# Convolution and gated feed-forward on one core: gate and up weights transposed by DMA, and the convolution's rows rounded on ScalarE

## What is computed

```python
K = 2.0 * einsum('hn,hnl->hl', Ct, exp(P)).real        # one long filter per head, length 1024
y = irfft(rfft(x) * rfft(K)) + x * D                    # causal convolution
y = y * (arange(L) < length)                            # mask
def qlinear(x, w):                                      # both sides rounded to 8-bit levels
    s = max(abs(t)) / 127; q = round(t / s) * s         # per row of x, per output row of w
    return einsum('bsh,oh->bso', xq, wq)
out = x + qlinear(silu(qlinear(y, w_gate)) * qlinear(y, w_up), w_down)
```

## Time and profile before

| what | value |
|---|---|
| median of 3 runs | 1317.04 us |
| the profiled execution | 1316.23 us |
| its span in the trace | 1313.0 us |
| TensorE busy | 1242.5 us, 95% |
| VectorE busy | 915.2 us, 70% |
| ScalarE busy | 408.7 us, 31% |
| GpSimd busy | 339.5 us, 26% |
| packets of the DMA queue, as a share of 16 engines | 45.3% of the span |

### The profile page before, as it was taken

The page is one execution under the profiler, slowest core; times in us unless marked ns, Lnnn a source line. Parts: engine busy times, 40 slices in busy tenths (PEclk is TensorE's granted clock), DMA queues, the critical chain, the costliest instruction groups (busy, mean ns, idle before and its releaser), DMA issues.

```text
span 1313.0 us, 19670 instructions
## 1 busy us (share of the span) xinstructions
PE 1242.5 (95%) x6581; PEld 675.8 (51%) x6676; DVE 915.2 (70%) x1542; ACT 408.7 (31%) x595; POOL 339.5 (26%) x318
## 2 busy tenths in 40 slices
PE   2499999999997999999999999999999999999997
PEld 0377777776763444444444444444444444444443
DVE  7578888888876577765677755677756677756675
ACT  2244454445531322222322222222222222222222
POOL 2133344325530321121221121221121221122220
PEclk9999999999998999999999999999999999999999
DMA  3279999998962233322223322323322323322322
GB/s 100 86 227 283 288 278 296 290 300 251 305 211 83 43 72 78 86 62 70 69 69 78 86 62 70 70 68 81 83 62 70 70 68 83 81 62 70 70 63 78
DMA packets 137593, 161.51 MB, mean 123 GB/s; under 512 B 101644, under 2 KB 101854, under 8 KB 136286
## 3 DMA queue, kind: packets, MB, share of 16 engines
q1 hardware_dynamic: 137566, 161.16, 45.3%
HBM read 113.28 MB, written 25.49 MB: 106 GB/s over the span
## 4 chain that ended last, share of the span: by engine, by line
PE 68%; issue 0%; DVE 0%; ACT 0%
PE ps_g L1055 23%; PE ps_u L1055 23%; PE ps_o L1081 22%; PE ps_o L1088 1%; PE ps_t L1065 0%; ACT h_t L1190 0%; DVE ps_o L1142 0%; DVE res L1145 0%
## 5 line engine op out<-in xcount | busy, mean ns | idle before, releaser
L1219 POOL TENSOR_TENSOR h_int<-h,rounder 128x512 bf16<-128x512 f32 x186 | 174.4, 952 | 703.3 <-ACT h L1181 700.6
L1055 PE MATMUL ps_g<-wgu,rows 128*128 128x512 bf16 (+1 forms) x1516 | 327.1, 358 | 5.9 <-PEq L405 4.9
L1055 PE MATMUL ps_u<-wgu,rows 128*128 128x512 bf16 (+1 forms) x1493 | 324.7, 357 | 2.3
L1081 PE MATMUL ps_o<-wd,h_t 128*128 128x512 bf16 x1314 | 294.0, 379 | 1.8 <-issue 0.2
L1175 ACT ACTIVATE g_buf<-g_buf 128x512 f32<-128x512 f32 x192 | 112.3, 585 | 584.1 <-DVE g_buf L1113 584.1
L1113 DVE SCALAR_TENSOR_TENSOR g_buf<-ps_g,sx_all,wide 128x512 f32<-128x512 f32 x192 | 132.3, 689 | 229.6 <-PE ps_g L1055 229.6
L846 PE MATMUL ps_y<-u,toep 128*128 128x512 f32 (+7 forms) x1024 | 266.2, 413 | 2.3 <-ACT s_rows L715 0.9
L1055 PEld LDWEIGHTS ps_g<-wgu,rows 128*128 128x128 bf16 x1536 | 145.2, 98 | 163.5 <-issue 13.2
L1055 PEld LDWEIGHTS ps_u<-wgu,rows 128*128 128x128 bf16 x1536 | 147.1, 98 | 151.8 <-issue 1.4
L846 PEld LDWEIGHTS ps_y<-u,toep 128*128 128x128 f32 x1024 | 177.6, 192 | 89.6 <-issue 57.5
L1081 PEld LDWEIGHTS ps_o<-wd,h_t 128*128 128x128 bf16 x1346 | 131.0, 98 | 151.9 <-issue 1.1
(11 more groups left out here) (140 smaller groups left out, 623.1 us busy)
## 6 DMA issues: line engine op xcount, KB each, us to landing
toep<-k_rev SPq DMA_DIRECT2D x64, 512.0 KB, 6.4
res<-in_x SPq DMA_DIRECT2D x64, 256.0 KB, 3.9
out_x<-res SPq DMA_DIRECT2D x64, 256.0 KB, 3.2
wide<-in_L_ffn_w_gate SPq DMA_DIRECT2D x22, 512.0 KB, 6.8
wide<-in_L_ffn_w_up SPq DMA_DIRECT2D x22, 512.0 KB, 8.7
wide<-in_L_ffn_w_down SPq DMA_DIRECT2D x8, 1376.0 KB, 7.5
rows<-in_x SPq DMA_DIRECT2D x32, 256.0 KB, 6.8
x_more<-in_x SPq DMA_DIRECT2D x32, 256.0 KB, 7.0
```

Of the source, the lines that this page charges most:

```text
L1055: last = pe.matmul(bank[:, 0:n], xq[:, par, c, :], wgu[:, NC - 1 - c, first + cols.start:first + cols.stop], start=(c == 0), stop=(c == NC ...
L1081: last = pe.matmul(ps_o[o][:], h_t[0:width, c, :], wd[0:width, c, o * W:(o + 1) * W], start=(c == 0), stop=(c == FC - 1))
L1219: pool.tensor_tensor(h_int[:, piece(j)], h[:, par, piece(j)], rounder[:].to_broadcast([P, n]), ALU.subtract).then_inc(h_int_ready, 1)
```

## The change

Gate and up weights: the 16 transposes of TensorE in each gate iteration and the two ScalarE copies (L863, L676) go. In their place SyncE issues two DMA transposes (`move_w`), each of one half of `w_int` (128 x 1024 bf16, eight blocks, 256 KB) straight into `wgu`. Each is put ahead of the load of the same half for iteration i+2. GpSimd waits for the DMA's semaphore `w_moved[k]` in place of TensorE's. The down weights are handled as before, with piece numbers of their own.

Output rows of the convolution: VectorE keeps the multiplication (`y_scaled`) and loses the rounding. ScalarE does it in two steps (`round_y`): `y + ROUND` in place, 128 x 1024 f32, then `- ROUND` into `xq`. They stand last in ScalarE's iteration.

```diff
+            def move_w(i, k):
+                sp.wait_ge(w_int_ready, pieces(i, k) + 1)
+                first = row_of(i) + k * F
+                sp.dma_start_transpose(wgu[:, :, first:first + P], w_int[:, k * L:(k + 1) * L]).then_inc(w_moved[k], 16)
+
             def body(i, par):
                 if gate_stage(i):
+                    move_w(i, 0)
                     if has(i, GU_ITERS - 2):
-                        sp.wait_ge(w_int_ready, pieces(i, 0) + 1)
                         load_gu(i + 2, par, 0)
...
-                if gate_stage(i) and has(i, GU_ITERS - 2):
-                    sp.wait_ge(w_int_ready, pieces(i, 1) + 1)
-                    load_gu(i + 2, par, 1)
+                if gate_stage(i):
+                    move_w(i, 1)
+                    if has(i, GU_ITERS - 2):
+                        load_gu(i + 2, par, 1)
...
+            for k in range(2):
+                sp.wait_ge(w_moved[k], 16 * GU_ITERS)
...
-                if turned is not None:
-                    pool.wait_ge(w_turned, turned)
+                if gate_stage(i):
+                    if not isinstance(i, int) or i >= 1:
+                        pool.wait_ge(w_moved[k], 16 * i)
...
+            def round_y(i, par):
+                v = y[:, par].rearrange("p c h b -> p (c h b)")
+                act.wait_ge(y_scaled, i + 1)
+                act.activation(v, v, ACT.Copy, bias=ROUND).then_inc(y_rounded, 1)
+                act.wait_ge(y_rounded, i + 1)
+                if not isinstance(i, int) or i >= 1:
+                    act.wait_ge(xq_stored, 16 * i)
+                act.activation(xq[:].rearrange("p c t -> p (c t)"), v, ACT.Copy, bias=-ROUND).then_inc(xq_ready, 1)
...
             def place_w(i, par, k):
-                act.wait_ge(w_turned, pieces(i, k) + 1)
-                if gate_stage(i):
-                    dst = wgu[:, :, bass.ds(row_of(i) + k * F, P)]
-                    act.activation(dst, ps_w[k][:], ACT.Copy).then_inc(w_placed, 1)
-                    return
+                act.wait_ge(w_turned, down_pieces(i, k) + 1)
...
+                if not isinstance(i, int) or i >= 1:
+                    round_y(i - 1, 1 - par)
...
                 dve.tensor_tensor(v, v, ps_i[:].unsqueeze(1).to_broadcast([P, NC, P]), ALU.mult).then_inc(y_scaled, 1)
-                dve.wait_ge(y_scaled, i + 1)
-                if not isinstance(i, int) or i >= 1:
-                    dve.wait_ge(xq_stored, 16 * i)
-                dve.tensor_scalar(xq[:], v, ROUND, ROUND, ALU.add, ALU.subtract).then_inc(xq_ready, 1)
...
-                    if gate_stage(i) or down_stage(i):
-                        turn_w(i, par, hh if gate_stage(i) else 2 * hh)
+                    if not gate_stage(i) and down_stage(i):
+                        turn_w(i, par, 2 * hh)
```

More of the change, by code:

```diff
@@ L453, in convolve_and_pack @@
         w_int_ready = sem("w_int_ready")
+        w_moved = [sem(f"w_moved{k}") for k in range(2)]
         w_turned = sem("w_turned")
@@ L517, in run @@
             stage[0] = "down"
[L518 to L521, removed]
+            body(DOWN_FIRST, DOWN_FIRST % 2)
+            with eng.Fori(DOWN_FIRST + 1, WEIGHT_ITERS - 4, 2) as i:
+                body(i, 1 - DOWN_FIRST % 2)
+                body(i + 1, DOWN_FIRST % 2)
+            for i in range(WEIGHT_ITERS - 3, TILES):
                 body(i, i % 2)
@@ L606, in store_scales @@
                     sp.wait_ge(s_stored, 80)
-            run(sp, body, lambda: store_scales(0))
+            for i in range(DOWN_FIRST):
+                body(i, i % 2)
+            store_scales(0)
+            for k in range(2):
+                sp.wait_ge(w_moved[k], 16 * GU_ITERS)
+            for i in range(DOWN_FIRST, TILES):
+                body(i, i % 2)
             sp.wait_ge(xq_stored, 16 * TILES)
@@ L623, in unround @@
                     src, out = w_f32[:, down_half(par)][:, cols], w_int[:, cols]
-                if turned is not None:
-                    pool.wait_ge(w_turned, turned)
+                if gate_stage(i):
+                    if not isinstance(i, int) or i >= 1:
+                        pool.wait_ge(w_moved[k], 16 * i)
+                else:
+                    if k < 2 and isinstance(i, int) and i == DOWN_FIRST:
+                        pool.wait_ge(w_moved[k], 16 * GU_ITERS)
+                    if not isinstance(i, int) or i > DOWN_FIRST:
+                        pool.wait_ge(w_turned, down_pieces(i - 1, k) + 1)
                 if not gate_stage(i) and k == BATCHES - 1:
@@ L630, in unround @@
                                    ALU.subtract).then_inc(w_int_ready, 1)
-            unround(0, 0, 0, None)
+            unround(0, 0, 0)
             def body(i, par):
                 if gate_stage(i):
[L636 to L644, removed]
+                    unround(i, par, 1)
+                    if has(i, GU_ITERS - 1):
+                        unround(i + 1, 1 - par, 0)
+                else:
+                    if down_stage(i):
+                        unround(i, par, 2)
+                    if has(i, WEIGHT_ITERS - 1):
+                        unround(i + 1, 1 - par, 0)
+                        unround(i + 1, 1 - par, 1)
             run(pool, body)
@@ L721, in _ @@
             run(act, body)
+            round_y(TILES - 1, (TILES - 1) % 2)
         @block.vector
@@ L850, in turn_w @@
             def turn_w(i, par, k):
[L852 to L853 removed]
+                m = down_pieces(i, k)
+                pe.wait_ge(w_int_ready, pieces(i, k) + 1)
                 if not isinstance(i, int) or m >= 2:
                     pe.wait_ge(w_placed, m - 1)
[L857 to L861 removed]
+                cols = turn_cols(k)
+                bank, start, stop = ps_w[(BATCHES * down_slot(par) + k) % 2], cols.start, cols.stop
                 for c, f in enumerate(range(start, stop, P)):
@@ L891, in body @@
                             turn_x(1 - par, k)
-                    if gate_stage(i) or down_stage(i):
-                        turn_w(i, par, hh if gate_stage(i) else 2 * hh)
-                        if hh == 0 and not gate_stage(i):
+                    if not gate_stage(i) and down_stage(i):
+                        turn_w(i, par, 2 * hh)
+                        if hh == 0:
                             turn_w(i, par, 1)
```

19 lines of the change are left out of this document (4 added, 15 removed).

## The result

| | before | after |
|---|---|---|
| median | 1316.22 us (4 runs, 1314.43 to 1324.29) | 1330.03 us (4 runs, 1328.06 to 1330.83) |
| ratio after / before, 95% interval | | 1.0095 (1.0056 to 1.0133) |
| span of the profiled execution | 1313.0 us | 1328.2 us |

The change costs 14 us by the medians, and 7 to 18 us by the interval of the ratio. I had forecast 1362, at least 1332. The sign was right, the size was wrong by a factor of three. And the loss isn't where I put it.

What follows compares the result with a forecast made beforehand. TensorE sets the gate stage's pace and the DMA engines barely keep up; transposes +46.6 us, load margins -3, stage end +2.2, down stage 0: +45.8 us, giving 1362 us, range 1332 to 1404.

Steps and rivals of the forecast that it cites:

- The engines have 0.2 us of room, so the period grows to 10.05 + 2.65 - 0.2 = 12.5 us: Gate stage: DMA engines nearly full, so two transposes lengthen each of iterations 3 to 21, 46.6 us in all.
- Only that no wait shows: Gate stage: the only evidence named for room in the DMA queue, on which a faster kernel (1300.6 us, chance 0.07) rested.
- The draw: Gate stage rival: the queue gives some, the period stays at 10.05 us, 1319 us in all; chance 0.05.
- the sign that I had named against myself: Gate stage: a period under 10.1 us in the changed profile would prove the forecast wrong on the queue.
- The price of a transpose: Gate stage: 0.166 us of all DMA engines a block, so 2.65 us for the 16 blocks added to each iteration.
- The removed 0.89 us is therefore worth nothing: Gate stage: TensorE's saving in each iteration brings no time, as it waits for loads in the longer period.
- ScalarE has room, and `xq` 1.5 us later only shrinks SyncE's pause: Each iteration: ScalarE, busy 51.55 of 100.82 us, can take the rounding; later `xq` only shortens SyncE's 5.5 us pause.
- The down stage keeps its work: 0: Down stage, behind the gate iterations: the change was booked as costing no time there.
- The tail, +2.2: End of the down stage, tile 31: two rounding steps and a wait for tile 30's store add 2.2 us.
- The clock: Gate stage rival: idle TensorE runs slow convolutions, two an iteration, +101 us, 1417 us; chance 0.05.
- The range: Whole kernel: 1332 to 1404 us, taking in the lower transpose price and dearer transposes, leaving out the other rivals.
- The least price of the transposes: Gate stage: lower end, their bytes at 285 GB/s, 1.84 us an iteration, +31 us.

Runs made afterwards that it cites:

- e7: Kernel before plus two DMA transposes of `w_int` into the still unused `wd` in each gate iteration, nothing removed; 1320.8 us, ratio 1.0019.
- e2: Kernel before with only the DMA transposes of the change, the rounding left on VectorE in one step; 1319.6 us, ratio 1.0001.
- e5: Changed kernel with each DMA transpose issued twice, the first of the two into `wd`, GpSimd waiting for both; 1415.8 us, ratio 1.0738.
- e4: Changed kernel with the loads of `x` put ahead of the first transpose on SyncE's queue in the gate stage; 1330.2 us, ratio 1.0082.
- e3: Kernel before with only the rounding moved to ScalarE, the transposes left on TensorE; 1332.7 us, ratio 1.0104.
- e9: Kernel before with only the rounding moved to ScalarE, and the `s_rows` scale copies put ahead of it; 1323.4 us, ratio 1.0051.
- e1: Changed kernel with the `s_rows` scale copies put ahead of `round_y` on ScalarE in iterations 22 and 30; 1324.2 us, ratio 1.0037.
- e10: Changed kernel with ScalarE rounding only tiles 0 to 21 and VectorE rounding tiles 22 to 31; 1319.7 us, ratio 1.0017.

## Why the prediction was wrong

- **"The engines have 0.2 us of room, so the period grows to 10.05 + 2.65 - 0.2 = 12.5 us"** is the step that failed. The period stayed at 10.0 to 10.1, and e7 shows the room by itself: two more transposes, the same period. 46.6 us fell away. I had read a share of 1.00 as full, and the landings of 7 to 9 us as a backlog. The engines then moved 331 to 338 GB/s in three kernels. Over such a stretch the share went to 1.08 or 1.09 and no further, at 338 and at 301 GB/s. "Only that no wait shows" was what I held to speak for room, and it was the best evidence there was. The page "SBUF — State Buffer" of the Trainium skill (A bandwidth-pool intuition that's wrong) gives 436 GB/s for DMA traffic on the on-chip memory. No long stretch here came to it, and the highest slice of the profile after is 349; but the 1.87 us from 289.33 on moved 429 GB/s in the changed kernel, so the figure isn't out of reach. It would have warned me that 285 need not be full.
- **"The draw", 0.05**, was what the gate stage did, with its own number: it "needs 339 GB/s", and the windows show 336. Its mechanism, that the queue gives some and TensorE's saving is spent, is what came, as did the sign that I had named against myself, a period under 10.1 us. That its 1319 us is within 1 us of e2 is luck: the 2 us in it were for ScalarE's rounding at the end, which e2 hasn't, and e2 came there by a gain of 3.1 and a loss of 7.2 us.
- **The price of a transpose**: 1.33 us was an engine time, and in the period it was nothing where queue and SyncE had room (e7) and 2 us where SyncE had no pause left (e5). The issue was put at 1.23 us; it was 1.23 to 3.55 us in the changed kernel. Of SyncE I had said "no bound", and in e5 its issues fill the period. At the stage's end a long issue stood ahead of a load of `x`, for a 3 us wait. The prediction also read the page "DMA: Bandwidth & Descriptors" of the Trainium skill (Latency and other measured facts) as speaking of the destination; the page says "non-contiguous mid-dim" and not on which side. No run here tells the two kinds apart.
- **"The removed 0.89 us is therefore worth nothing"**: right, but for another reason. 0.79 and 0.49 us of waits for `x` took it, and where those were moved away (e4) a late gate load took it by way of VectorE. In the first iterations, which I had called cheap, some of it came through, for 3 us.
- **ScalarE has room, and `xq` 1.5 us later only shrinks SyncE's pause**: right in the gate stage (5.5 us became 2.7), wrong in the down stage. I counted ScalarE's busy time (half of a stretch of the gate stage) and didn't follow its order: the rounding waits for VectorE, and what stands behind it waits too. Two copies of 0.25 us were worth 7 to 9 us (e3 against e9, by ratios and by medians).
- **"The down stage keeps its work: 0"**: its work, yes. It measured +19.0 us, 8.8 of them by the order of the copies (e1 against after), most of the rest by later `x`.
- **The tail, +2.2**: 15.75 us from the last convolution's start to the next stage for 15.27 before, +0.5.
- **The clock** was a rival for the gate stage. It came in single places and not once an iteration: the two slow convolutions of 7.1 us, as the earlier trace rows had one, that of 5.80 us at 257.98, and the transposes and the convolution behind the wait of 3.03 us.
- **The range** had no case in which a cost lies outside the gate stage. The least price of the transposes, their bytes at 285 GB/s (+31 us), gives 1347; the end at 1332 lies 15 us below that and has no sum of its own. That the transposes could be free in time and the loss lie elsewhere had no case, and that 1330.03 came near that end is luck.

## What to carry to other kernels

A DMA share near 1.00 with long landings and no waits is no proof of a full queue; ask with extra transfers that nobody needs, and look whether the engine that issues them still has pauses. When an engine gets an operation that waits for another engine, look at each thing that stands behind it in its program, in every stage and in the rare iterations above all; its busy share says nothing on that. A time saved in a stage with several limits near each other is spent by the next one, and the order of loads at the joint of two stages is worth a look by itself.

## What the hardware showed that I had not expected

- An operation of VectorE beside one of GpSimd stretches: the `diag` step took 1.98 us at 186.84, beside GpSimd's of 1.89 that began at the same time, and takes 0.29 us alone. In e2 the rounding took 1.60 us for 0.69, begun 0.85 us behind one of GpSimd's of 1.89 us:

```profile
191.70 1.60 DVE L805 TENSOR_SCALAR xq<-y 128x1024 bf16<-128x1024 f32 x1
```

  The page "SBUF — State Buffer" of the Trainium skill (SBUF: two separate sides) says that some forms of VectorE operations and GpSimd share a pair of ports that one of them holds for a whole instruction. The trace agrees for these two forms: both ended within 0.6 us of GpSimd's end. VectorE's `tensor_tensor` ahead of the rounding, which also lay beside GpSimd's, kept its 1.21 us.
- A share of 1.07 to 1.09 stood beside 273, 301, 331 and 338 GB/s.
- The issue of a DMA transpose took SyncE between 1.23 and 4.60 us over all runs. Its length goes with the distance from the start of the transpose ahead: in e7, mostly 4.1 to 6.3 us behind it, the median was 1.25 us, and in e5 those 1.28 to 1.55 us behind it took 3.7 to 4.6. That isn't all: the 3.55 us at 278.82 and the 4.19 us of e10 came 6.5 us behind.
- After a wait of 3.5 to 3.9 us the next convolution ran at a granted clock of 0.57 or 0.58 (300.24 to 307.20 and 395.69 to 402.70) and took 7.1 us for 4.2, so that a wait 3 us longer than before cost 5.9. After the wait of 3.03 us the transposes of `x` ran at 0.50 (289.33 to 291.20).
